# A language-model tower on one core: gate rows multiplied ahead of the up projection, products kept in PSUM, 24 of 33 expert pairs in three-pass form

## The chip, the core and the metric

The kernel runs on one core of one Trainium2 chip. Its engines work side by side, each through its own queue in order: TensorE (PE) multiplies matrices into PSUM, VectorE (DVE) and ScalarE (ACT) work on SBUF and PSUM, GpSimd (POOL) works on SBUF alone, and SyncE (SP) issues DMAs. PSUM has eight banks of 128 rows x 512 floats, and this kernel uses all eight. The metric is the device time of one execution in microseconds (us).

## What is computed

Eight batches of 512 tokens pass through an embedding, one attention-like block and a mixture-of-experts layer. Cut to what matters here:

```python
h = concat([fine_w[ids], softmax(cluster_logits[ids]) @ coarse_w])      # 128 wide
h = h + attn(layernorm(h))     # rms norms, decayed scores, gelu
def ffn(x):                    # x = layernorm(h)
    p = softmax(x @ router_w.T + bias)
    topk_p, topk_i = top_k(p, 6)                  # of 64 experts, capacity-limited
    out = sum over chosen experts e: gate[e] * ((silu(x @ w_gate[e].T) * (x @ w_up[e].T)) @ w_down[e].T)
    return out + shared experts' mean             # 2 shared experts, each 64 wide
h = h + ffn(layernorm(h))
```

The kernel computes all 64 routed experts for every token and multiplies by a gate that is zero where an expert was not chosen.

## The kernel before, in words

Experts are taken in pairs, two times 64 hidden rows on the 128 partitions: pair 0 holds the two shared experts, pairs 1 to 32 the routed ones. One batch is a sequence of 33 iterations, one per pair p, written out on every engine by the functions `pe_sequence`, `act_sequence`, `dve_sequence` and `pool_sequence`. There is no scheduler: the order on each engine is the order of the Python code.

For pair p, PE makes the gate projection (three matmuls into `bank_g`, L481 to L483: high x high, low x high, high x low halves, fp32r) and the up projection (three into `bank_u`). ACT takes silu of the gate bank into `hid` (`act_silu`, L623). DVE multiplies by the up bank (`dve_up`, L881), POOL multiplies by the gate rows, one gate per token, that a DMA has spread over the partitions (L1040). Four iterations later (`LAG`) PE multiplies with the down weights into `bank_y` (`down`). There are two forms of this. In the plain form (even pairs) it is one fp32 matmul from `hid` (L467), which the hardware runs as two records. In the split form (odd pairs) ACT first copies `hid` rounded to fp32r into `hid_hi` (`act_hi`, L629), DVE subtracts to get the rest, `hid_lo` (`dve_lo`, L887), and PE makes three fp32r matmuls (L461, L462, L464).

While the pairs of batch b pass, the steps of the next batches stand between them, at iterations fixed by the tables `DVE_AT`, `PE_AT`, `ACT_AT` and `POOL_AT`: the attention and router of batch b+1 (the "late" steps) and the embedding of batch b+2 (the "early" ones). Those of which the text speaks:

- iteration 6: DVE `scores` (L725), which PE's `state` matmuls (L378) wait for;
- iterations 9 and 10: ACT `squares` (L593); iteration 10: ACT's exp of the cluster logits (early), which puts an activation table load before and after it;
- iteration 11: DVE `xn2` (L746), which PE's transposes `xn2_t` (L396) of iteration 12 wait for;
- iteration 17: DVE `h2` and the statistics after it; iteration 18: POOL `inv3` (L1016); iteration 19: DVE `x3` (L769); iteration 20: PE's transposes of it (L414);
- iterations 23 to 30: the router. PE's matmul is at 23, the logits on DVE (L779 to L785) and ACT's exp with its two table loads at 24, probabilities, top 6 and gates on DVE at 26 to 29, PE's transposes at 30.

Batches 0 to 6 have late steps within their sequence, batches 0 to 5 also early ones, the last has neither. In batches 1 to 5 POOL also issues four gathers, at iterations 1 to 4.

A bank is used again when its reader is done: the gate bank of pair p waits for the silu of p-2, and the up bank for `up_used` of p-2.

## Time and profile before

| what | value |
|---|---|
| median of 3 runs | 717.83 us (716.76 to 718.17) |
| span of the profiled execution | 716.0 us |
| PE busy | 692.8 us, 97% of the span |
| DVE busy | 523.4 us, 73% |
| POOL busy | 466.5 us, 65% |
| ACT busy | 350.6 us, 49% |
| granted TensorE clock, mean | 0.995 |

The only time known of the profiled execution is its span, 716.0 us from its first to its last instruction; the median of the runs is 1.8 us above that. Busy time of PE overlaps from one matmul to the next, so distances between starts tell more than durations do.

### The profile page before, as it was taken

How to read it: one execution, taken by the hardware profiler on the slowest of the kernel's cores; microseconds unless marked ns; L12 is line 12 of the kernel's file. 1: busy time of each engine (PE TensorE's matmuls, PEld its weight loads, DVE VectorE, ACT ScalarE, POOL GpSimd, SP SyncE). 2: the span in 40 equal slices, each digit the busy share in tenths (PEclk: the TensorE clock that was granted, in tenths of full speed). 3: DMA queues.
4: the chain of work that ended last, by engine and by line, in shares of the span. 5: the costliest groups of instructions: out<-in, count | busy, mean ns of one | idle time of the engine just before them, and what ended most of it. 6: DMA issues, size and time to landing. Idle time of an engine off the chain costs nothing.

```text
span 716.0 us, 9975 instructions
## 1 busy us (share of the span) xinstructions
PE 692.8 (97%) x3133; PEld 524.7 (73%) x3133; DVE 523.4 (73%) x1074; ACT 350.6 (49%) x609; POOL 466.5 (65%) x345
## 2 busy tenths in 40 slices
PE   7788899999999999999999999999999999999998
PEld 7666677777777777777777777777777777777775
DVE  5677686987768867887769877788678766674444
ACT  3543455446454374445553474544745435534432
POOL 5035477776677767685676776676775656676664
PEclk9999999999999999999999999999999999999999
DMA  5504232243323333333333433333333433334431
GB/s 204 226 1 128 71 118 104 85 133 105 111 106 114 114 108 99 120 113 102 118 103 101 128 103 103 118 110 109 114 105 102 125 103 105 115 112 124 138 123 60
DMA packets 48869, 80.17 MB, mean 112 GB/s; under 512 B 9520, under 2 KB 13744, under 8 KB 48816
## 3 DMA queue, kind: packets, MB, share of 16 engines
q1 hardware_dynamic: 47792, 77.44, 33.4%
q0 software_dynamic: 1024, 2.10, 1.2%
q8 instruction: 25, 0.41, 0.2%
q14 instruction: 28, 0.23, 0.1%
HBM read 76.35 MB, written 3.15 MB: 111 GB/s over the span
## 4 chain that ended last, share of the span: by engine, by line
PE 88%; DVE 4%; issue 3%; POOL 2%; ACT 1%; DVEq 0%; POOLq 0%
PE bank_y L467 16%; PE bank_g L481 8%; PE bank_g L482 8%; PE bank_g L483 8%; PE bank_u L483 8%; PE bank_u L481 8%; PE bank_u L482 8%; PE bank_y L464 4%; PE bank_y L462 4%; PE bank_y L461 4%; POOL hid L1040 1%; PE bank_f L408 1%; PE bank_f L386 1%; PE bank_f L402 1%; PE bank_f L445 1%
## 5 line engine op out<-in xcount | busy, mean ns | idle before, releaser
L1040 POOL TENSOR_TENSOR hid<-hid,gate_rows 128x512 f32<-128x512 f32 x256 | 374.2, 1470 | 195.4 <-DVE hid L881 193.0
L623 ACT ACTIVATE hid<-bank_g 128x512 f32<-128x512 f32 x264 | 156.6, 599 | 264.4 <-PE bank_g L483 261.8
L881 DVE TENSOR_TENSOR hid<-hid,bank_u 128x512 f32<-128x512 f32 x264 | 178.7, 681 | 128.3 <-PE bank_u L483 78.2
L481 PE MATMUL bank_g<-x_hi,gate_hi 128*128 128x512 f32 x264 | 142.9, 541 | 0.0
L467 PE MATMUL bank_y<-hid,w_down 128*128 128x512 f32 x272 | 138.7, 591 | 0.0
L887 DVE TENSOR_TENSOR hid_lo<-hid,hid_hi 128x512 fp32r<-128x512 f32 x128 | 110.2, 861 | 2.4 <-ACT hid_hi L629 2.4
L482 PE MATMUL bank_g<-x_hi,gate_lo 128*128 128x512 f32 x264 | 104.5, 396 | 0.0
L483 PE MATMUL bank_g<-x_lo,gate_hi 128*128 128x512 f32 x264 | 104.5, 396 | 0.0
L481 PE MATMUL bank_u<-x_hi,up_hi 128*128 128x512 f32 x264 | 103.9, 393 | 0.1
L483 PE MATMUL bank_u<-x_lo,up_hi 128*128 128x512 f32 x264 | 103.8, 393 | 0.0
L482 PE MATMUL bank_u<-x_hi,up_lo 128*128 128x512 f32 x264 | 103.8, 393 | 0.0
L629 ACT ACTIVATE hid_hi<-hid 128x512 fp32r<-128x512 f32 x128 | 80.3, 628 | 5.5 <-POOL hid L1040 4.8
L481 PEld LDWEIGHTS bank_g<-x_hi,gate_hi 128*128 128x128 f32 x264 | 50.1, 190 | 24.1 <-issue 19.2
L482 PEld LDWEIGHTS bank_g<-x_hi,gate_lo 128*128 128x128 f32 x264 | 50.2, 190 | 23.9 <-issue 19.2
L467 PEld LDWEIGHTS bank_y<-hid,w_down 128*128 128x128 f32 x272 | 51.1, 188 | 11.3
L481 PEld LDWEIGHTS bank_u<-x_hi,up_hi 128*128 128x128 f32 x264 | 49.8, 189 | 12.4 <-DVE hid L881 0.6
L482 PEld LDWEIGHTS bank_u<-x_hi,up_lo 128*128 128x128 f32 x264 | 49.8, 189 | 11.8
L483 PEld LDWEIGHTS bank_g<-x_lo,gate_hi 128*128 128x128 f32 x264 | 49.7, 188 | 11.6
L483 PEld LDWEIGHTS bank_u<-x_lo,up_hi 128*128 128x128 f32 x264 | 49.8, 189 | 11.1
L461 PE MATMUL bank_y<-hid_hi,down_hi 128*128 128x512 f32 x128 | 51.3, 401 | 0.0
L464 PE MATMUL bank_y<-hid_lo,down_hi 128*128 128x512 f32 x128 | 50.8, 397 | 0.0
L462 PE MATMUL bank_y<-hid_hi,down_lo 128*128 128x512 f32 x128 | 50.6, 395 | 0.0
(209 smaller groups left out, 857.1 us busy)
## 6 DMA issues: line engine op xcount, KB each, us to landing
gate_rows<-gates_dram SPq DMA_DIRECT2D x512, 128.0 KB, 2.9
w_down<-down_t_dram SPq DMA_DIRECT2D x3, 704.0 KB, 14.5
out_dram<-later SPq DMA_DIRECT2D x7, 256.0 KB, 3.1
hid<-gate_t_dram SPq DMA_DIRECT2D x2, 704.0 KB, 5.8
gates_dram<-gates_t SPq DMA_DIRECT2D x8, 128.0 KB, 2.2
gate_rows<-up_t_dram SPq DMA_DIRECT2D x1, 704.0 KB, 5.7
later<-up_t_dram SPq DMA_DIRECT2D x1, 704.0 KB, 9.9
raw<-gate_t_dram SPq DMA_DIRECT2D x1, 704.0 KB, 11.0
```

The source lines that it names most:

```text
L461: pe.matmul(y, down_hi[:, j, :], hid_hi[:, k, :], start=False, stop=False)
L462: pe.matmul(y, down_lo[:, j, :], hid_hi[:, k, :], start=False, stop=False)
L464: pe.matmul(y, down_hi[:, j, :], hid_lo[:, k, :], start=False, stop=False).then_inc(sem("down_done"), 1)
L467: pe.matmul(y, w_down[:, p, :], hid[:, slot(par, p), :], start=(p == 0), stop=(p == PAIRS - 1)).then_inc(sem("down_done"), 1)
L481: pe.matmul(o, w_hi[name][:, p, :], x3_hi[par][:, :], start=True, stop=False)
L482: pe.matmul(o, w_lo[name][:, p, :], x3_hi[par][:, :], start=False, stop=False)
L483: pe.matmul(o, w_hi[name][:, p, :], x3_lo[par][:, :], start=False, stop=True).then_inc(sem("pe_" + name), 1)
L623: act.activation(hid[:, slot(par, p), :], bank_g[(p + par) % 2][:, :], ACT.Silu).then_inc(sem("silu"), 1)
L629: act.activation(hid_hi[:, (p // 2) % SPLIT_RING, :], hid[:, slot(par, p), :], ACT.Copy)\
L881: dve.tensor_tensor(hid[:, s, :], hid[:, s, :], bank_u[(p + par) % 2][:, :], ALU.mult)\
L887: dve.tensor_tensor(hid_lo[:, k, :], hid[:, slot(par, p), :], hid_hi[:, k, :].bitcast(F32), ALU.subtract)\
L1040: pool.tensor_tensor(hid[:, s, :], hid[:, s, :], gate_rows[:, row, :], ALU.mult)\
```

## The change

Twenty-four pairs instead of sixteen take the split form: all but 0 to 4, 17, 25, 27 and 29. For these pairs the order of the two products is turned round: POOL multiplies the silu by the gate rows as soon as the silu is there, without the up bank, and DVE then multiplies that by the up bank and writes the product back into the same bank (`dve_product`). ACT rounds it from there to `hid_hi`, DVE subtracts from there to `hid_lo`. The up bank of a split pair is therefore held until `hid_lo` is made; there are three up banks instead of two, and one accumulator `bank_y` instead of two. The first down matmul of a batch waits for the copy of the last batch's result, moved from ACT's iteration 5 to 4. `hid_hi` and `hid_lo` have three slots instead of two. The step `x1` goes from DVE to ACT, with a bias column that POOL makes in two small operations. Some SBUF tensors are merged to make room.

```diff
-SPLIT_LAG, SPLIT_RING = 2, 2
-SPLITS = PAIRS // 2
+SPLIT_RING = 3
+PLAIN_PAIRS = (0, 1, 2, 3, 4, 17, 25, 27, 29)
+SPLIT_PAIRS = tuple(p for p in range(PAIRS) if p not in PLAIN_PAIRS)
...
-        bank_u = [bank(f"bank_u{i}") for i in range(2)]
-        bank_y = [bank(f"bank_y{i}") for i in range(2)]
+        bank_u = [bank(f"bank_u{i}") for i in range(3)]
+        bank_y = bank("bank_y")
...
+        def split_slot_freed(b, p):
+            n = SPLITS * b + split_index(p) - SPLIT_RING
+            return PAIRS * (n // SPLITS) + SPLIT_PAIRS[n % SPLITS] + 1 if n >= 0 else 0
...
+            if p == 0:
+                wait(pe, "ffn_t", b)
...
+            for name, o in (("gate", bank_g[q % 2][:, :]), ("up", bank_u[q % 3][:, :])):
+                if name == "gate":
+                    wait(pe, "silu", q - 1)
+                else:
+                    b3, p3 = pairs_back(b, p, 3)
+                    if b3 is not None and is_split(p3):
+                        pe.wait_ge(sem("hid_lo"), split_count(b3, p3))
+                    elif b3 is not None:
+                        pe.wait_ge(sem("up_used"), plain_count(b3, p3))
...
+            if p == ACT_AT["x1"]:
+                act.wait_ge(sem("shift1"), b + 1)
+                wait(act, "x2", b)
+                for t in range(TILES):
+                    last = act.activation(x1[:, t, :], emb[par][:, t, :], ACT.Identity,
+                                          bias=shift1[:, t:t + 1], scale=inv1[:, 0, t:t + 1])
...
+        def act_hi(act, b, p):
+            act.wait_ge(sem("product"), split_count(b, p))
+            wait(act, "down_done", split_slot_freed(b, p))
+            act.activation(hid_hi[:, split_slot(b, p), :], bank_u[(PAIRS * b + p) % 3][:, :], ACT.Copy)\
...
-                if p >= SPLIT_LAG and is_split(p - SPLIT_LAG):
-                    act_hi(act, b, par, p - SPLIT_LAG)
+                b1, p1 = pairs_back(b, p, 1)
+                if b1 is not None and is_split(p1):
+                    act_hi(act, b1, p1)
...
+        def dve_product(dve, b, p):
+            q = PAIRS * b + p
+            dve.wait_ge(sem("gated"), q + 1)
+            dve.wait_ge(sem("pe_up"), q + 1)
+            u = bank_u[q % 3][:, :]
+            dve.tensor_tensor(u, hid[:, slot(b % 2, p), :], u, ALU.mult).then_inc(sem("product"), 1)
...
+        def dve_split(dve, b, p):
+            b2, p2 = pairs_back(b, p, 2)
+            if b2 is not None and is_split(p2):
+                dve_lo(dve, b2, p2)
+            b1, p1 = pairs_back(b, p, 1)
+            if b1 is not None and is_split(p1):
+                dve_product(dve, b1, p1)
...
             for p in range(PAIRS):
+                dve_split(dve, b, p)
...
-                if p >= AHEAD - 1 or not first:
+                if (p >= AHEAD - 1 or not first) and not is_split(p):
                     dve_up(dve, b, par, p)
-                if p >= SPLIT_LAG and is_split(p - SPLIT_LAG):
-                    dve_lo(dve, b, par, p - SPLIT_LAG)
...
-                pool.wait_ge(sem("up_used"), q + 1)
+                if is_split(p):
+                    pool.wait_ge(sem("silu"), q + 1)
+                else:
+                    pool.wait_ge(sem("up_used"), plain_count(b, p))
```

How this stands on the engines is shown at three places. The first is DVE at iterations 10 and 11 of batch 3. Before, with L893 the output of batch 2, L881 the products of pairs 10 and 11 with the up bank, L746 the step `xn2`, L887 the rest of pair 9:

```order
L881 TENSOR_TENSOR hid<-hid,bank_u1 128x512 [waits pe_up,silu]
L887 TENSOR_TENSOR hid_lo<-hid,hid_hi 128x512 [waits hid_hi]
L893 TENSOR_TENSOR later<-bank_f0,later 128x512 [waits stored,pe_out]
L881 TENSOR_TENSOR hid<-hid,bank_u0 128x512 [waits pe_up,silu]
L746 TENSOR_SCALAR xn<-shared,inv2 128x128 [waits inv2]
L746 TENSOR_SCALAR xn<-shared,inv2 128x128 x3
```

and in the changed kernel, where L941 makes `hid_lo` of pairs 8 and 9, L936 the products of pairs 9 and 10, and L792 is `xn2`:

```order
L941 TENSOR_TENSOR hid_lo<-bank_u2,hid_hi 128x512 [waits hid_hi]
L936 TENSOR_TENSOR bank_u0<-hid,bank_u0 128x512 [waits pe_up,gated]
L956 TENSOR_TENSOR later<-bank_f0,later 128x512 [waits stored,pe_out]
L941 TENSOR_TENSOR hid_lo<-bank_u0,hid_hi 128x512 [waits hid_hi]
L936 TENSOR_TENSOR bank_u1<-hid,bank_u1 128x512 [waits pe_up,gated]
L792 TENSOR_SCALAR xn<-shared,inv2 128x128 [waits inv2]
L792 TENSOR_SCALAR xn<-shared,inv2 128x128 x3
```

`xn2` stood behind a product that waits for the silu of pair 10 and the up bank; it now stands behind the `hid_lo` of pair 9 and a product that waits for `gated`, POOL's multiplication of pair 10.

The second place is ACT at iterations 9 and 10 of a batch with early steps. Before, L623 is the silu (of pairs 9, then 10 and 11), L629 `hid_hi` of pair 7, L593 the squares, L612 the exp:

```order
L623 ACTIVATE hid<-bank_g0 128x512 [waits down_done,pe_gate]
L629 ACTIVATE hid_hi<-hid 128x512 [waits down_done,gated]
L593 ACTIVATE shared,ss2<-shared 128x128 [waits x2]
L593 ACTIVATE shared,ss2<-shared 128x128
L612 ACT_TABLE_LOAD
L612 ACTIVATE lg<-lg 128x256 [waits cluster_logits]
L623 ACT_TABLE_LOAD [waits down_done]
L623 ACTIVATE hid<-bank_g1 128x512 [waits pe_gate]
L623 ACTIVATE hid<-bank_g0 128x512 [waits down_done,pe_gate]
```

In the changed kernel L675 is the silu, L681 `hid_hi` (of pairs 8 and 9), L645 the squares, L664 the exp:

```order
L675 ACTIVATE hid<-bank_g0 128x512 [waits down_done,pe_gate]
L681 ACTIVATE hid_hi<-bank_u2 128x512 [waits down_done,product]
L645 ACTIVATE shared,ss2<-shared 128x128 [waits x2]
L645 ACTIVATE shared,ss2<-shared 128x128
L664 ACT_TABLE_LOAD
L664 ACTIVATE lg<-lg 128x256 [waits cluster_logits]
L675 ACT_TABLE_LOAD [waits down_done]
L675 ACTIVATE hid<-bank_g1 128x512 [waits pe_gate]
L681 ACTIVATE hid_hi<-bank_u0 128x512 [waits down_done,product]
L675 ACTIVATE hid<-bank_g0 128x512 [waits down_done,pe_gate]
```

The `hid_hi` before the squares is that of pair 8 instead of pair 7, and one of pair 9 stands between the silus of pairs 10 and 11.

The third place is DVE at iterations 17 to 19. Before, L764 ends the statistics of `h2`, L881 is the product of pairs 17, 18 and L769 is `x3`:

```order
L764 TENSOR_SCALAR var3<-mv3 128x4 [waits mv3]
L881 TENSOR_TENSOR hid<-hid,bank_u1 128x512 [waits pe_up,silu]
L887 TENSOR_TENSOR hid_lo<-hid,hid_hi 128x512 [waits hid_hi]
L868 BN_AGGR mv1<-bn1 128x2 [waits bn1]
L868 BN_AGGR mv1<-bn1 128x2 x3
L872 TENSOR_SCALAR var1<-mv1 128x4 [waits mv1]
L873 TENSOR_SCALAR var1<-mv1 128x4
L881 TENSOR_TENSOR hid<-hid,bank_u0 128x512 [waits pe_up,silu]
L769 TENSOR_SCALAR xn<-later,mv3,inv3 128x128 [waits inv3]
```

In the changed kernel L927 is the plain product of pair 17, L936 that of pair 18, L815 `x3`:

```order
L810 TENSOR_SCALAR var3<-mv3 128x4 [waits mv3]
L927 TENSOR_TENSOR hid<-hid,bank_u2 128x512 [waits pe_up,silu]
L941 TENSOR_TENSOR hid_lo<-bank_u1,hid_hi 128x512 [waits hid_hi]
L914 BN_AGGR mv1<-bn1 128x2 [waits bn1]
L914 BN_AGGR mv1<-bn1 128x2 x3
L918 TENSOR_SCALAR var1<-mv1 128x4 [waits mv1]
L919 TENSOR_SCALAR var1<-mv1 128x4
L936 TENSOR_TENSOR bank_u0<-hid,bank_u0 128x512 [waits pe_up,gated]
L815 TENSOR_SCALAR xn<-later,mv3,inv3 128x128 [waits inv3]
```

The instruction ahead of `x3` waits for POOL's multiplication of pair 18, which stands behind `inv3` in POOL's queue.

## Rows read from the trace of the kernel before

**Rows 1.** The page, part 4: shares of the chain that ended last.
```profile
PE 88%; DVE 4%; issue 3%; POOL 2%; ACT 1%; DVEq 0%; POOLq 0%
```

**Rows 2.** Windows: one batch (busy us by engine, clock, DMA share, GB/s).
```profile
389.94:472.98 83.04, 82.55 (x367) 62.07 (x366) 65.02 (x131) 43.01 (x75) 57.74 (x43) 1.00 0.36 110
```

**Rows 3.** Timeline of PE, pairs 9 to 11: start, us, engine, line, operation.
```profile
333.53 0.40 PE L461 MATMUL bank_y<-hid_hi,down_hi 128*128 128x512 f32 x1
...
334.23 0.39 PE L481 MATMUL bank_g<-x_hi,gate_hi 128*128 128x512 f32 x1
...
335.60 1.02 PE L467 MATMUL bank_y<-hid,w_down 128*128 128x512 f32 x2
...
336.69 0.40 PE L482 MATMUL bank_g<-x_hi,gate_lo 128*128 128x512 f32 x1
```

**Rows 4.** Groups of instructions: busy us, mean ns | idle before.
```profile
L881 DVE TENSOR_TENSOR hid<-hid,bank_u 128x512 f32<-128x512 f32 x264 | 178.7, 681 | 128.3 <-PE bank_u L483 78.2 <-ACT hid L623 48.7
...
L887 DVE TENSOR_TENSOR hid_lo<-hid,hid_hi 128x512 fp32r<-128x512 f32 x128 | 110.2, 861 | 2.4 <-ACT hid_hi L629 2.4
...
L774 DVE TENSOR_TENSOR x_lo<-bank_f,x_hi 128x512 fp32r<-128x512 f32 x8 | 5.5, 692 | 6.1 <-ACT x_hi L604 6.1
...
L604 ACT ACTIVATE x_hi<-bank_f 128x512 fp32r<-128x512 f32 x8 | 4.7, 593 | 0.0
```

**Rows 5.** Timeline of ACT, iteration 10: squares, table load, silus of pairs 10, 11.
```profile
334.06 0.30 ACT L593 ACTIVATE shared<-shared 128x128 f32<-128x128 f32 x1
...
334.76 1.28 ACT L612 ACT_TABLE_LOAD   x1
336.05 0.42 ACT L612 ACTIVATE lg<-lg 128x256 f32<-128x256 f32 x1
...
337.78 1.09 ACT L623 ACTIVATE hid<-bank_g 128x512 f32<-128x512 f32 x2
```

**Rows 6.** Timelines of DVE and PE, iterations 11 and 12: xn2 and its transposes.
```profile
339.02 1.93 DVE L746 TENSOR_SCALAR xn<-shared,inv 128x128 f32<-128x128 f32 x4
...
341.23 0.60 PE L396 MATMUL bank_f<-ident,xn 128*128 128x128 f32 x4
```

**Rows 7.** Timelines of four engines, iterations 16 to 20: silu, h2, gate multiplication, inv3, x3, transposes.
```profile
351.07 0.60 ACT L623 ACTIVATE hid<-bank_g 128x512 f32<-128x512 f32 x1 [0.97 <-PE bank_g L483]
...
353.50 0.75 DVE L752 SCALAR_TENSOR_TENSOR h<-bank_f,op_mul,shared 128x512 f32<-128x512 f32 x1 [0.99 <-PE bank_f L408]
...
356.57 1.66 POOL L1040 TENSOR_TENSOR hid<-hid,gate_rows 128x512 f32<-128x512 f32 x1 [2.70 <-DVE hid L881]
358.18 1.01 POOL L1016 TENSOR_TENSOR inv<-var,neg_half 128x4 f32<-128x4 f32 x1
...
359.23 2.09 DVE L769 TENSOR_SCALAR xn<-h,mv,inv 128x128 f32<-128x128 f32 x4 [0.33 <-POOL inv L1016]
...
361.96 0.60 PE L414 MATMUL bank_f<-ident,xn 128*128 128x128 f32 x4
```

**Rows 8.** Timelines of PE, DVE and ACT, iterations 23 to 26: router, silu 24, gate 26.
```profile
368.83 1.00 PE L419 MATMUL bank_f<-cols,xn_t 128*128 128x64 f32 x8
...
369.86 0.42 DVE L779 TENSOR_TENSOR turns<-bank_f,rows 128x256 f32<-128x256 f32 x1
...
370.78 0.44 DVE L785 TENSOR_TENSOR turns<-turns,rstat 128x256 f32<-128x256 f32 x1
...
372.98 1.09 ACT L623 ACTIVATE hid<-bank_g 128x512 f32<-128x512 f32 x2
...
374.04 0.39 PE L481 MATMUL bank_g<-x_hi,gate_hi 128*128 128x512 f32 x1
```

**Rows 9.** Timelines of POOL, DVE and PE, iterations 4 to 6: gate multiplication, scores, state.
```profile
321.38 1.29 POOL L1040 TENSOR_TENSOR hid<-hid,gate_rows 128x512 f32<-128x512 f32 x1
...
324.22 0.74 DVE L725 TENSOR_TENSOR shared<-bank_f,decay_mask 128x256 f32<-128x256 f32 x2
...
325.06 0.91 PE L378 MATMUL bank_f<-z,shared 128*128 128x128 f32 x6 [0.49 <-issue]
```

More of the change, by code:

```diff
@@ L18 @@
+import itertools
 from contextlib import ExitStack
@@ L463, in down @@
                 pe.wait_ge(sem("hid_lo"), split_count(b, p))
-                pe.matmul(y, down_hi[:, j, :], hid_lo[:, k, :], start=False, stop=False).then_inc(sem("down_done"), 1)
+                pe.matmul(y, down_hi[:, j, :], hid_lo[:, k, :], start=False, stop=(p == PAIRS - 1)).then_inc(sem("down_done"), 1)
             else:
@@ L675, in _ @@
                     act.wait_ge(sem("w_down"), 16 * (PAIRS // CHUNK))
-                    act.activation(down_hi[:, :, :], odd_pairs(w_down), ACT.Copy).then_inc(sem("down_hi"), 1)
+                    for j, pairs in split_runs():
+                        last = act.activation(down_hi[:, j, :], w_down[:, pairs, :], ACT.Copy)
+                    last.then_inc(sem("down_hi"), 1)
                     act.wait_ge(sem("sigmoid"), 1)
@@ L681, in _ @@
             last = BATCHES - 1
-            for p in range(PAIRS - SPLIT_LAG, PAIRS):
-                if is_split(p):
-                    act_hi(act, last, 1, p)
+            if is_split(PAIRS - 1):
+                act_hi(act, last, PAIRS - 1)
             act.wait_ge(sem("down_done"), PAIRS * BATCHES)
@@ L982, in _ @@
             last = BATCHES - 1
-            for p in range(PAIRS - SPLIT_LAG, PAIRS):
-                if is_split(p):
-                    dve_lo(dve, last, 1, p)
+            dve_split(dve, last, PAIRS)
+            if is_split(PAIRS - 1):
+                dve_lo(dve, last, PAIRS - 1)
             dve.wait_ge(sem("stored"), 16 * BATCHES)
```

108 lines of the change are left out of this document (58 added, 50 removed).

## The prediction

> **What bounds the kernel now.** I read three views in this order: the chain of waits, to see which engine it stays on; the busy times of one batch, to see what that engine loses; then the timelines around every place where PE takes something from another engine, to see how late that could come. The chain is on PE for 88% of the span, with no second engine over 4% [rows 1]. A middle batch takes 83.04 us and PE works in 82.55 of them, at the full granted clock, the 2.4 GHz level; DVE works 65 and POOL 58 [rows 2]. So a microsecond of PE work is worth a microsecond, and so is a microsecond of PE waiting, which nothing gives back. The change pays in the first and has to be charged for the second.
>
> **What it saves.** A split down product is three matmuls 0.23 us apart (333.53 to 334.23), 0.70 in all. A plain one and the first gate matmul behind it take 335.60 to 336.69, that is 1.09, less 0.23 is 0.86 [rows 3]. Twenty-four pairs are split instead of sixteen, and each of the eight saves 0.16: 8 x 8 batches x 0.16 = 10.2 us.
>
> **What the engines get.** Eight `hid_lo` more per batch go to DVE, and four `x1` leave it. A `hid_lo` took 0.86 on average with both inputs in SBUF; with one input in PSUM the nearest row is `x3_lo`, 0.69 [rows 4]. I use 0.69 for the product and for `hid_lo`. [...] The product writes PSUM, which no row of DVE shows; the nearest is the same operation into SBUF, 0.68, and I let it lie between 0.55 and 0.86. In a run of split pairs DVE cannot take the next product before the last `hid_lo`, and that waits for ACT: product 0.69, rounding 0.59 [rows 4], 0.60 from one DVE start to the next, hand-overs of 0.04 (inv3 ends at 359.19, `x3` starts at 359.23 [rows 7]): 1.96 us per pair against PE's 2.08 (nine matmuls). It holds, by 0.12; at 0.86 it would lose 0.05 a pair, some 10 us over 192 pairs. The four `x1` lie in ACT's idle time of iteration 5 at 0.30 each (nearest row, the squares [rows 5]); POOL's two small operations are well under its 25 idle us of a batch [rows 2]. The copy of `bank_y` lies beside the gate and up matmuls of pair 4. I cost these at zero; `x1` uncovered would be 1.2 us in seven batches, 8 us.
>
> **What it charges: order.** DVE takes the product of pair p-1 first thing in iteration p and waits there for POOL. Before, it needed silu and the up bank only. After a silu's end come POOL (1.29 alone [rows 9]), the product (0.60 to the next start) and two hand-overs, so a step of iteration p can start 2.0 us after silu p-1, where it started 0.6 after it. The steps and PE's uses of them keep their iterations, so each use must have that much slack. I take a middle batch, put the changed kernel's PE on the old clock, and look at the four uses.
>
> - *`xn2_t`, iteration 12.* `hid_hi` of pair 8 has the slot of pair 5, whose down product is the last of iteration 9 and ends 0.16 after 334.23 [rows 3]. So it starts at 334.44, the squares at 334.94 instead of 334.06 (ACT starts every 0.5), and the exp and its two table loads push the silu of pair 10 from 337.78 to 338.66 [rows 5]. It ends 339.26, POOL 340.60, product from 340.65, `xn2` from 341.25. It took 1.93 with one of its four pieces stopped by POOL: end 343.2. PE used it at 341.23 [rows 6], now 341.07: 2.1 late. With none stopped I put it at 1.2 (four at the 0.30 of a 128x128 piece on ACT [rows 5]), 1.4 late; each piece behind one more POOL operation gives 3.7. I take 1.9, in the six batches with early steps: 11.4 us.
> - *`x3_t`, iteration 20.* Silu 16 ends at 351.67 [rows 7], POOL 353.01, product, `h2` from 353.66 at the earliest instead of 353.50. To the end of inv3 it was 5.69, now 5.32, as POOL is not stopped (1.66 to 1.29). Then `x3` does not start at 0.04 after it, but behind gate multiplication and product of pair 18, another 1.29 + 0.05 + 0.60: 360.9 instead of 359.23. With 2.09 it ends at 363.0; PE wants it at 361.96 [rows 7] less three shorter down products, 361.48. Late by 1.5; by 0.6 if `x3` runs in 1.2; by 2.9 if gelu's table loads in iteration 14 still hold up `h2`. I take 1.7 in six batches, 1.0 in batch 6: 11.2 us.
> - *Router to gates, iterations 24 to 30.* The down product of pair 19 ends at 368.99 [rows 8] and frees the slot for `hid_hi` 22: 369.04 to 369.63, `hid_lo` 22, product 23 at 370.28, logits from 370.88 instead of 369.86. Silu 24 goes from 372.98 to 374.0, ends 374.6; gate 26 wants it at 374.04 less 0.16: 0.77 late. Behind silu 24 stands `hid_hi` 23, then `hid_lo` 23 (to 375.83), which the up bank of pair 26 waits for: 1.3 late in all. In iterations 26 to 29 DVE has three more such steps between the `hid_lo`, and I add 1.05, between 0 and 2. 2.35 in seven batches: 16.5 us.
> - *`state`, iteration 6.* POOL, full of gathers, ends pair 4 at 322.67, then pair 5 at 324.01; the product puts `scores` from 324.22 to 324.66, and PE already waits for them [rows 9]. 0.45 in batches 1 to 5: 2.2 us; between 0 and 4.
>
> The exp and its load in the first of these chains start 1.29 apart [rows 5]. The Trainium skill (ScalarE: Activation LUTs, "What ACT_TABLE_LOAD costs") has 1.28 for the load and 1.38 more for a drain, which would put silu 10 and 24 later still. The trace has no such drain, so it decides against the rule; the sum above goes by the row.
>
> **Sum.** -10.2 + 11.4 + 11.2 + 16.5 + 2.2 = +31.1. On the profiled span of 716.0 that is 747.1; the median of the runs lies 1.8 above the span, so **749 us**. The lower bounds (1.4 x 6, 0.6 x 7, 0.77 x 7, 0) come to 18.0 - 10.2 = +8, 726 us; the upper (3.7 x 6, 2.9 x 7, 3.3 x 7, 4) to 69.6 - 10.2 = +59, 777.
>
> **Rivals.**
> - *All of it hidden: faster.* If DVE, free of POOL's stops, is early enough at all four uses, only the saving stays: 717.8 - 10.2 = 708. For it: three up banks give PE a lead of three pairs, and the DVE-ACT loop fits. Against it: this needs slack of 1.4 us at each use, and the trace has 0.3 at `xn2` (ends 340.95, used 341.23) and 0.6 at `x3` (361.32, 361.96). It decides where the waits of a batch come to less than 10.2 / 7, about 1.5 us. Chance 0.15, for all of 708 to 716.4.
> - *The waits overlap: a small loss.* If a wait at one use gives the other engines the lead that the next use needs, the lower bounds hold, about 726. For it: after each wait of PE the others catch up. Against it: the uses are 8 and 4 iterations apart, and each chain starts from PE's own work. 0.20 for 716.4 to 733, 0.04 of it within 0.2% of before.
> - *POOL stops every piece: a larger loss.* POOL now starts at the silu, so its operations come back to back where `xn2` and `x3` run, and each of the four pieces waits for one: upper bounds, about 777. For it: one piece of `xn2` was stopped even before, and `x3` took 2.09 [rows 6, 7]. The Trainium skill (SBUF — State Buffer, "SBUF: two separate sides") calls the shared ports an exclusive lock, held for the whole instruction; the rows bear that out. Against it: while PE waits, POOL soon has nothing left to do. 0.13, above 766.
> - The forecast, 733 to 766: 0.52.
>
> **Chances and range.** A measurement of this kernel can tell about 0.2% from no change. Faster 0.15, within 0.2% 0.04, slower 0.81. The range is 717 to 775: it leaves out the first rival and some 0.05 of the third.
>
> **What would show it.** Right: a middle batch of some 87 to 89 us; idle time of PE before `xn2_t`, `x3_t` and `state` and before the gate and up matmuls of pairs 26 and 29, put down to DVE and ACT; `hid_lo` at 0.69 throughout; POOL's multiplication near 1.3. Wrong: PE busy through a batch of 82 us; or waits in the runs of split pairs without steps, which the last batch shows alone: there PE should take 1.3 us less than now, and if it takes more, the product into PSUM is dearer than I think.

## The result, and the profile after

The changed kernel takes **781.9 us** (median of 4 runs, 781.1 to 784.0) against 718.0 beside it: 1.089 times as long, 95% interval 1.087 to 1.092. Forecast were 749, with a range from 717 to 775. The sign and the kind of loss were right, the size was not: 64 us instead of 31.

The profiled execution has a span of 781.8 us, 65.8 more than before. Its chain of waits no longer stays on PE; a quarter of it is POOL, and four fifths of that is one line, the gate multiplication (L1108, 20% of the chain) [rows 1]:

```profile
PE 35%; issue 33%; POOL 25%; DVE 4%; ACT 2%; DMA 1%; POOLq 0%; SPq 0%; DVEq 0%; ACTq 0%
```

One middle batch and the last one, in the columns of [rows 2], and below them the last batch of the kernel before. The middle batch has grown from 83.04 to 92.24; in it PE is at the full clock (1.00), and idle for 8.4 us. The last batch, which has no steps, has grown from 69.67 to 70.10.

```profile
429.11:521.35 92.24, 83.86 (x375) 62.80 (x374) 65.06 (x135) 48.25 (x87) 51.70 (x45) 1.00 0.34 99
702.22:772.32 70.10, 69.17 (x284) 52.87 (x283) 39.07 (x61) 33.59 (x57) 42.17 (x33) 1.00 0.45 126
```

```profile
636.67:706.34 69.67, 69.67 (x277) 51.51 (x276) 32.12 (x50) 27.96 (x49) 48.11 (x33) 1.00 0.40 126
```

The groups that answer to [rows 4], from the page: POOL's multiplication, `hid_hi`, `hid_lo` and the product. All four take what was forecast (1.3, 0.59, 0.69, 0.69), so none of these durations explains the loss. What has changed is the last column, the idle time ahead of them: before, DVE's product never waited for POOL and `hid_lo` waited 2.4 us in all for ACT; now it is 70.9 and 115.1.

```profile
L1108 POOL TENSOR_TENSOR hid<-hid,gate_rows 128x512 f32<-128x512 f32 x256 | 328.3, 1295 | 272.5 <-ACT hid L675 182.3
L681 ACT ACTIVATE hid_hi<-bank_u 128x512 fp32r<-128x512 f32 x192 | 114.8, 598 | 213.5 <-DVE bank_u L936 188.8
L941 DVE TENSOR_TENSOR hid_lo<-bank_u,hid_hi 128x512 fp32r<-128x512 f32 x192 | 132.1, 688 | 117.2 <-ACT hid_hi L681 115.1
L936 DVE TENSOR_TENSOR bank_u<-hid,bank_u 128x512 f32<-128x512 f32 x192 | 132.1, 688 | 71.6 <-POOL hid L1108 70.9
```

What PE waited for (total us, times, longest): `xn2` (L432), the up banks (L525), `x3` (L450), the gate banks, and for `state` (L414). The number of times is telling: 8 is once a batch, at one place.

```profile
PE bank_f L432 <- DVE xn L792: 17.3, 8, 2.5
PE bank_u L525 <- DVE hid_lo L941: 15.9, 34, 1.0
PE bank_f L450 <- DVE xn L815: 10.3, 8, 1.4
PE bank_g L525 <- ACT hid L675: 7.4, 12, 0.8
PE bank_f L414 <- issue: 7.0, 6, 1.2
```

The next table goes by place. PE's second gate matmul starts once in each pair; the table has the distances between these starts in one middle batch, summed over the stretches around each use. "Best" is the run e18 below, in which no stretch of such a batch has a wait of any size.

| us, middle batch | before | after | best |
|---|---|---|---|
| pairs 0 and 1 | 4.77 | 6.00 | 4.78 |
| 4 to 7 (`state`) | 12.99 | 14.01 | 12.63 |
| 11 and 12 (`xn2_t`) | 5.20 | 8.92 | 5.19 |
| 19 and 20 (`x3_t`) | 4.78 | 6.84 | 4.66 |
| 21 to 32 (router, gates) | 27.31 | 29.28 | 26.99 |
| the rest | 27.97 | 27.18 | 27.01 |
| sum | 83.03 | 92.23 | 81.26 |

**The largest loss, at `xn2`.** Timelines of ACT, DVE, POOL and PE in iterations 8 to 12 of one batch; a row with x4 is four instructions together, [ ] the idle time before it.

```profile
458.80 0.60 ACT L681 ACTIVATE hid_hi<-bank_u 128x512 fp32r<-128x512 f32 x1 [0.86 <-PE bank_y L502]
...
459.99 1.28 ACT L664 ACT_TABLE_LOAD   x1
461.29 0.42 ACT L664 ACTIVATE lg<-lg 128x256 f32<-128x256 f32 x1
...
463.02 0.60 ACT L675 ACTIVATE hid<-bank_g 128x512 f32<-128x512 f32 x1
```

```profile
465.02 0.70 DVE L936 TENSOR_TENSOR bank_u<-hid,bank_u 128x512 f32<-128x512 f32 x1 [0.19 <-POOL hid L1108]
465.62 3.34 DVE L792 TENSOR_SCALAR xn<-shared,inv 128x128 f32<-128x128 f32 x4
```

```profile
463.69 2.55 POOL L1108 TENSOR_TENSOR hid<-hid,gate_rows 128x512 f32<-128x512 f32 x2 [2.20 <-ACT hid L675]
466.19 1.27 POOL L1073 TENSOR_TENSOR shared<-emb,shared 128x512 f32<-128x512 f32 x1
467.42 1.27 POOL L1108 TENSOR_TENSOR hid<-hid,gate_rows 128x512 f32<-128x512 f32 x1
```

```profile
469.01 0.66 PE L432 MATMUL bank_f<-ident,xn 128*128 128x128 f32 x4 [2.47 <-DVE xn L792]
```

The chain ahead of `xn2` is the one forecast, link by link: `hid_hi` 8 waits for a slot that PE frees, the exp and its two table loads (1.28 each) follow, the silu, POOL, the product. `xn2` starts 0.60 after the product, as it should. But it takes 3.34 instead of 1.93 [rows 6]. Its four pieces run 465.62 to 466.32, then to 467.54, to 468.76 and to 468.96; each of the first three ends 0.08 after an operation of POOL does (466.24, 467.46, 468.68), and only the last takes its own 0.27. POOL, which now starts at the silu, has four operations back to back, `hx` (L1073) among them, and here one piece of DVE gets through per operation.

**The loss that was not foreseen, at pair 0.** DVE, POOL and PE at the end of one batch:

```profile
427.14 0.70 DVE L936 TENSOR_TENSOR bank_u<-hid,bank_u 128x512 f32<-128x512 f32 x1 [2.04 <-POOL hid L1108]
...
427.92 1.27 DVE L874 TENSOR_TENSOR_SCAN taken<-one_col,taken_end,bank_f 64x512 f32<-64x512 f32 x1
429.23 0.69 DVE L879 SCALAR_TENSOR_TENSOR gates_t<-taken,bank_f 64x512 f32<-64x512 f32 x1
429.95 0.69 DVE L941 TENSOR_TENSOR hid_lo<-bank_u,hid_hi 128x512 fp32r<-128x512 f32 x1
```

```profile
424.58 3.79 POOL L1108 TENSOR_TENSOR hid<-hid,gate_rows 128x512 f32<-128x512 f32 x3 [2.28 <-DVE hid L927]
```

```profile
430.69 0.50 PE L525 MATMUL bank_u<-x_hi,up_hi 128*128 128x512 f32 x1 [0.96 <-DVE hid_lo L941]
```

POOL takes its pairs in order, and the plain pair 29 still has to wait for DVE (2.28), so 30 and 31 are late; the product of 30 waits 2.04 for POOL, the scan `taken` and `gates_t` of iteration 31 stand behind it, and `hid_lo` 30, which frees the up bank of pair 0, behind those. The last batch waits there too, though it has no late steps, since the scan is the end of the batch before it.

At `x3` and `state` the shorter form of the same is seen [rows 7, 9]: `x3` starts behind a product (489.22) and takes 1.46; `scores` start at 448.38, behind a product that waited 3.51 for POOL, full of gathers, and PE's `state` waits 1.16.

```profile
489.22 0.70 DVE L936 TENSOR_TENSOR bank_u<-hid,bank_u 128x512 f32<-128x512 f32 x1 [2.18 <-POOL hid L1108]
489.82 1.46 DVE L815 TENSOR_SCALAR xn<-later,mv,inv 128x128 f32<-128x128 f32 x4
```

```profile
447.77 0.70 DVE L936 TENSOR_TENSOR bank_u<-hid,bank_u 128x512 f32<-128x512 f32 x1 [3.51 <-POOL hid L1108]
448.38 0.75 DVE L771 TENSOR_TENSOR shared<-bank_f,decay_mask 128x256 f32<-128x256 f32 x2
```

```profile
449.22 0.91 PE L414 MATMUL bank_f<-z,shared 128*128 128x128 f32 x6 [1.16 <-issue]
```

### The profile page after: what moved, and what is told of

Read it like the earlier page. It is cut to its first block, busy times and chain, and to the rows that moved or that the text cites. A ratio compares the mean times of both kernels' runs of the same rounds, so it can differ in the third digit from the quotient of the medians.

```text
span 781.8 us, 10340 instructions
## 1 busy us (share of the span) xinstructions
PE 705.5 (90%) x3197; PEld 535.8 (69%) x3197; DVE 530.0 (68%) x1110; ACT 395.5 (51%) x709; POOL 417.7 (53%) x361
## 4 chain that ended last, share of the span: by engine, by line
PE 35%; issue 33%; POOL 25%; DVE 4%; ACT 2%; DMA 1%; POOLq 0%; SPq 0%; DVEq 0%; ACTq 0%
POOL hid L1108 20%; PE bank_y L505 6%; PE bank_u L525 3%; PE bank_u L527 3%; PE bank_u L526 3%; PE bank_g L525 3%; PE bank_g L527 3%; PE bank_g L526 3%; PE bank_y L502 2%; PE bank_y L500 2%; PE bank_y L499 2%; DVE taken L874 1%; POOL inv L1082 1%; POOL shared L1073 1%; POOL inv L1076 1%
## 5 line engine op out<-in xcount | busy, mean ns | idle before, releaser
L1108 POOL TENSOR_TENSOR hid<-hid,gate_rows 128x512 f32<-128x512 f32 x256 | 328.3, 1295 | 272.5 <-ACT hid L675 182.3
L681 ACT ACTIVATE hid_hi<-bank_u 128x512 fp32r<-128x512 f32 x192 | 114.8, 598 | 213.5 <-DVE bank_u L936 188.8
L941 DVE TENSOR_TENSOR hid_lo<-bank_u,hid_hi 128x512 fp32r<-128x512 f32 x192 | 132.1, 688 | 117.2 <-ACT hid_hi L681 115.1
L675 ACT ACTIVATE hid<-bank_g 128x512 f32<-128x512 f32 x264 | 157.7, 598 | 92.2 <-PE bank_g L527 89.1
L936 DVE TENSOR_TENSOR bank_u<-hid,bank_u 128x512 f32<-128x512 f32 x192 | 132.1, 688 | 71.6 <-POOL hid L1108 70.9
L525 PE MATMUL bank_g<-x_hi,gate_hi 128*128 128x512 f32 x264 | 132.3, 501 | 7.4 <-ACT hid L675 7.4
L525 PE MATMUL bank_u<-x_hi,up_hi 128*128 128x512 f32 x264 | 109.2, 414 | 16.1 <-DVE hid_lo L941 15.9
L525 PEld LDWEIGHTS bank_u<-x_hi,up_hi 128*128 128x128 f32 x264 | 49.8, 189 | 45.0 <-DVE hid_lo L941 35.9
L499 PE MATMUL bank_y<-hid_hi,down_hi 128*128 128x512 f32 x192 | 76.7, 399 | 0.0
L500 PE MATMUL bank_y<-hid_hi,down_lo 128*128 128x512 f32 x192 | 76.5, 398 | 0.0
L502 PE MATMUL bank_y<-hid_lo,down_hi 128*128 128x512 f32 x192 | 76.1, 396 | 0.0
L505 PE MATMUL bank_y<-hid,w_down 128*128 128x512 f32 x144 | 73.4, 591 | 0.0
L525 PEld LDWEIGHTS bank_g<-x_hi,gate_hi 128*128 128x128 f32 x264 | 50.2, 190 | 30.6 <-ACT hid L675 13.3
L526 PEld LDWEIGHTS bank_g<-x_hi,gate_lo 128*128 128x128 f32 x264 | 50.3, 190 | 17.5 <-issue 12.0
L927 DVE TENSOR_TENSOR hid<-hid,bank_u 128x512 f32<-128x512 f32 x72 | 49.1, 682 | 12.9 <-PE bank_u L527 12.8
## 6 DMA issues: line engine op xcount, KB each, us to landing
w_down<-down_t_dram SPq DMA_DIRECT2D x3, 704.0 KB, 14.5
```

The lines of the kernel that those rows point to most:

```text
L499: pe.matmul(y, down_hi[:, j, :], hid_hi[:, k, :], start=False, stop=False)
L500: pe.matmul(y, down_lo[:, j, :], hid_hi[:, k, :], start=False, stop=False)
L502: pe.matmul(y, down_hi[:, j, :], hid_lo[:, k, :], start=False, stop=(p == PAIRS - 1)).then_inc(sem("down_done"), 1)
L505: pe.matmul(y, w_down[:, p, :], hid[:, slot(par, p), :], start=(p == 0), stop=(p == PAIRS - 1)).then_inc(sem("down_done"), 1)
L525: pe.matmul(o, w_hi[name][:, p, :], x3_hi[par][:, :], start=True, stop=False)
L526: pe.matmul(o, w_lo[name][:, p, :], x3_hi[par][:, :], start=False, stop=False)
```

## Experiments

Three theories: **order** (steps, and roundings that free a bank, stand on DVE behind a product that waits for POOL), **port** (pieces on DVE are stopped by POOL's operations, which now come back to back), **number** (24 split pairs are more than DVE and ACT carry). Times are medians, each against the kernel before on the same chip, which took 716.8 to 717.9 in all of them. A difference to the changed kernel (781.9) is one between chips, so some 1 us of it means nothing.

**e1, the step ahead of the split work.**
```diff
-                dve_split(dve, b, p)
                 if p == DVE_AT["result"] and not first:
                     dve_out(dve, b - 1, 1 - par)
...
                     dve_early(dve, b + 2, par, p, b // 2 + 2)
+                dve_split(dve, b, p)
```


> In each iteration DVE does its step first, and hid_lo of pair p-2 and the product of pair p-1 behind it; nothing else differs from the changed kernel (782). Theory A, order: the steps start late because they stand behind a product that waits for POOL. Then the waits at xn2_t, x3_t and state go for the most part and the time falls by 30 to 45, to 737 to 752; a part may come back as waits of the up banks for hid_lo, since the product now stands behind the step. Theory B, port: what makes xn2 and x3 late is that each of their pieces waits for one of POOL's back-to-back multiplications. Then an earlier start by some 0.7 us gives back only that, about 1 to 1.5 us a batch: 770 to 775. Theory C, number: 24 split pairs are more than DVE and ACT carry. Then the waits only move to the up banks and the time stays at 778 to 786.

762.2 us, 19.7 less, in none of the three ranges: the waits at pair 0 (4.75 in the table's first row) and `state` (12.63) are gone and those at `xn2` (6.46) and `x3` (5.78) about halved or better, but the router's stretch has grown to 31.42, and PE waits for up banks:

```profile
PE bank_u L525 <- DVE hid_lo L941: 34.2, 52, 2.6
```

Order is a cause, but it cannot be cured by turning it round: what frees a bank now stands behind the step.

**e2, POOL's `hx` away from `xn2`.**
```diff
-POOL_AT = dict(inv2=10, hx=12, inv3=18, inv1=20)
+POOL_AT = dict(inv2=10, hx=14, inv3=18, inv1=20)
```


> One number: POOL's operation hx moves from iteration 12 to 14, so that it no longer stands between the gate multiplications of pairs 11 and 12 while DVE has xn2. Theory B, port: one of the three pieces of xn2 that POOL stops is then not stopped, or the gate multiplication of pair 12 comes in its place 1.3 earlier; if not stopped, xn2 ends 1.3 to 1.9 earlier in six batches, 770 to 775. Theory A, order: the start of xn2 is what counts and it doesn't move; 779 to 783. If the next multiplication steps in hx's place, B gives 779 to 783 too, and the trace tells: xn2 then still has three pieces that end with a POOL operation.

767.3 us, 14.5 less for one number of a table, and less than the 770 to 775 that the port theory had allowed. `xn2` starts as late as it did (0.60 after the product) and takes 1.29: DVE, then POOL, whose next multiplication comes at 455.74, when `xn2` has ended.

```profile
453.98 1.29 DVE L792 TENSOR_SCALAR xn<-shared,inv 128x128 f32<-128x128 f32 x4
```

```profile
452.06 2.54 POOL L1108 TENSOR_TENSOR hid<-hid,gate_rows 128x512 f32<-128x512 f32 x2 [2.20 <-ACT hid L675]
455.74 1.29 POOL L1108 TENSOR_TENSOR hid<-hid,gate_rows 128x512 f32<-128x512 f32 x1 [1.14 <-ACT hid L675]
```

Port, at this use: one piece is still stopped, and two come free, not one, since the multiplication behind `hx` no longer meets them. PE's wait for `xn2` falls from 17.3 to 3.1 us in all.

**e3, the old order of the product, all else as changed.**
```diff
-            act.wait_ge(sem("product"), split_count(b, p))
+            act.wait_ge(sem("gated"), PAIRS * b + p + 1)
...
-                if is_split(p):
-                    pool.wait_ge(sem("silu"), q + 1)
+                pool.wait_ge(sem("up_used"), q + 1)
```


> All as in the changed kernel (24 split pairs, three up banks, one accumulator, x1 on ScalarE), but the product in the order of before: DVE multiplies with the up rows first, in place in SBUF, POOL multiplies the gate rows behind it, and hid_hi and hid_lo are made from hid in SBUF two iterations later. Theory A, order: the waits at pair 0, xn2, x3 and router vanish, and only the saving of eight split pairs a batch and a prelude 3 to 4 longer are left: 708 to 716. Theory C, number: 24 hid_lo at 0.86 and their ports stop POOL and make the gate multiplications late for the down products: 720 to 745. If the waits stay though the product does not wait for POOL, one accumulator or x1 is their cause: above 760.

729.8 us, 1.017 of before (1.015 to 1.019). The edit turns back several things together: the order of the two products, the rounding from PSUM instead of SBUF, the long hold of the up bank, `hid_hi` one iteration behind instead of two, and the split work at the head of DVE's iterations. The new order makes 52 of the 64 us with all that it brings along; this run does not price the parts. The 24 split pairs still do not pay, and the time lies in the range of the number theory (720 to 745). What is left is a wait at the router (stretch 29.65) and one at `xn2` (5.78). The chain, in three timelines: POOL's `inv1` holds up the gate multiplications of pairs 20 and 21, ACT's `hid_hi` 20 waits 1.68 for POOL, DVE's `hid_lo` 20 waits 1.50 for that, and behind it stand the logits (L822).

```profile
455.27 2.09 POOL L1076 TENSOR_TENSOR inv<-var,neg_half 128x8 f32<-128x8 f32 x1
...
458.03 5.95 POOL L1099 TENSOR_TENSOR hid<-hid,gate_rows 128x512 f32<-128x512 f32 x4
```

```profile
459.35 0.63 ACT L677 ACTIVATE hid_hi<-hid 128x512 fp32r<-128x512 f32 x1 [1.68 <-POOL hid L1099]
```

```profile
460.01 1.10 DVE L938 TENSOR_TENSOR hid_lo<-hid,hid_hi 128x512 fp32r<-128x512 f32 x1 [1.50 <-ACT hid_hi L677]
...
462.74 0.41 DVE L822 TENSOR_TENSOR turns<-bank_f,rows 128x256 f32<-128x256 f32 x1
```

**e4, the new order with 16 split pairs** (`PLAIN_PAIRS`: 0, 1, 2 and the even pairs 4 to 30).

> The changed kernel with 16 to 17 split pairs rather than 24: plain are 0, 1, 2 and then the even pairs 4 to 30, so 17 of 33 are plain and every second pair is split. Theory A, order: every second step still stands behind a product that waits for POOL, and the saving of 10 is lost; steps in an iteration behind a split pair wait as now. If the steps at 11 and 19 (behind pairs 10 and 18, both plain now) have their products out of the way, xn2 and x3 gain, and router (24, behind the split pair 23) does not: 750 to 775. Theory C, number: it is the density of the DVE and ACT work; all waits shrink, 725 to 735. Theory B, port: POOL still works back to back beside xn2: 780 to 790.

755.8 us, where the number theory had 725 to 735. The loss falls place by place: with pair 30 plain none at pair 0 (4.75), with 18 plain none at `x3` (4.76), but behind the split pairs 5 and 23 `state` (14.12) and the router (30.11) are as late as ever, and at `xn2` (6.78) POOL still meets the pieces. Order and port, not number.

**e5 and e6, rounding first, then the step, then the product; e6 with `hx` at 14 as well.**
```diff
-                dve_split(dve, b, p)
+                b2, p2 = pairs_back(b, p, 2)
+                if b2 is not None and is_split(p2):
+                    dve_lo(dve, b2, p2)
...
                     dve_early(dve, b + 2, par, p, b // 2 + 2)
+                b1, p1 = pairs_back(b, p, 1)
+                if b1 is not None and is_split(p1):
+                    dve_product(dve, b1, p1)
```


> Changed kernel, with DVE's order in an iteration: hid_lo of pair p-2, then the step, then the product of pair p-1. With the step ahead of both, PE waited 34 us in 52 places for up banks that hid_lo had not released; a bank is released here before the step. Theory A, order (nothing that waits for POOL may stand ahead of a step, nothing that releases a bank behind one): most of these 34 us go and the steps still start early, 730 to 745. Rival, number: the three up banks are short whatever the order, since product and hid_lo of a pair lie two iterations apart; then the waits stay near 30 us and the time at 755 to 762.

> The order hid_lo, step, product, and POOL's hx in iteration 14 rather than 12. Theory A and B together: hx beside xn2 cost 14 us in the changed kernel; here xn2 starts earlier, when POOL may have the multiplication of pair 10 or 11 in hand, so I expect half of it, 5 to 9 us under the same order with hx at 12. If the order alone brings xn2 clear of its use, hx is worth nothing: within 2.

795.7 and 789.0 us: worse than the changed kernel. My improvement of e1 was wrong. The product is now the last thing in an iteration and the rounding of the same pair the first of the next, so DVE stands idle for ACT's `hid_hi` between them and the step is late by that. In e1 and in the changed kernel the step, where there is one, lies between the two. In all DVE idles 145.5 us for `hid_hi` here, 115.1 in the changed kernel and 90.2 in e1. Without a step a pair takes the 1.96 us that the prediction had worked out, 0.66 of it idle (DVE's timeline of e5), and here a step comes on top:

```profile
476.72 0.69 DVE L941 TENSOR_TENSOR hid_lo<-bank_u,hid_hi 128x512 fp32r<-128x512 f32 x1 [0.66 <-ACT hid_hi L681]
477.33 0.69 DVE L936 TENSOR_TENSOR bank_u<-hid,bank_u 128x512 f32<-128x512 f32 x1
478.68 0.69 DVE L941 TENSOR_TENSOR hid_lo<-bank_u,hid_hi 128x512 fp32r<-128x512 f32 x1 [0.66 <-ACT hid_hi L681]
```

`hx` is worth 6.6 here, as expected.

**e7, e3 with `hid_lo` three iterations behind instead of two** (`pairs_back(b, p, 3)`).

> The order of before with 24 split pairs (729.8), but hid_lo made three iterations behind its pair rather than two; hid_hi stays at two. There PE lost about 1.4 us before the gate matmul of pair 25 and 1.3 before gates_t in seven batches, since hid_lo 20 and 21 stood ahead of the logits on DVE and waited for hid_hi, which waited for POOL. Theory A, order: a hid_lo that waits for nothing holds up no step; these 19 us go for the most part, 711 to 720. Rival, ports: POOL and DVE shut each other out (hid_lo with both inputs in SBUF took up to 1.4 us), whatever the order: 725 to 732.

752.5 us, a miss too: the down product is only four iterations behind, and PE now waits for the rounding itself.

```profile
PE bank_y L502 <- DVE hid_lo L938: 30.5, 37, 1.7
```

**e8, `x1` back on DVE, all else as changed** (the four `tensor_scalar` ahead of `xn_dec`).

> The changed kernel with x1 back on DVE in iteration 5, ahead of xn_dec; all else as changed. The prediction had x1 at zero on both engines. If that holds, only the prelude changes, where four x1 of 0.49 stand ahead of z on ScalarE: 779 to 783. If x1 on ScalarE holds up z and by it state (PE waits 0.7 there in five batches) it gains up to 4: 776 to 779. If the four x1 on DVE hold up scores, by 0.3 to 1.3 each where POOL shuts DVE out, PE waits longer for state: 785 to 795.

798.0 us, 16 more, above all that was expected. DVE's four pieces take 6.84 us there, beside two gathers and four multiplications of POOL; before, one took 728 ns on average, now 1371. The fourth alone takes 4.53: it begins at 451.29, within the second gather, and ends 0.09 after the last of the three multiplications behind that:

```profile
448.98 6.84 DVE L746 TENSOR_SCALAR x<-emb,mv,inv 128x128 f32<-128x128 f32 x4
```

```profile
450.92 1.05 POOL L1056 DMA_INDIRECT emb<-table_dram,idx  x1 [0.16 <-issue]
451.98 3.75 POOL L1104 TENSOR_TENSOR hid<-hid,gate_rows 128x512 f32<-128x512 f32 x3
```

So moving `x1` is a part of the change that pays, in the new order.

**e11, steps first in twelve iterations only** (0, 2, 4, 5, 6, 8 to 11, 19, 24, 31), `hx` at 14.

> The changed kernel with DVE's step ahead of hid_lo and product only in the iterations whose step PE soon needs (0, 2, 4, 5, 6, 8 to 11, 19, 24, 31), as in the changed kernel elsewhere, and hx in iteration 14. Theories A and B together: the waits at pair 0, state, xn2_t and x3_t go (1.2 + 0.7 + 2.7 + 1.6 a batch) without the up-bank waits of iterations 18 to 27 that the order with all steps first brought (some 4 a batch): 732 to 745. If the up-bank waits follow wherever a step goes first: 750 to 760.

752.4 us, the rival's range, though its mechanism is only half there. The waits at pair 0 (4.94) and `state` (12.65) are gone, and a new up-bank wait stands at pair 21 (0.60); but in all PE waits 17.5 us for up banks, against 17.2 in e2 with the same `hx`. The stretches at `x3` (6.73) and the router (29.37) are as long as in the changed kernel.

**e12, e3 with the 16 split pairs of e4.**

> Old order of the product and 16 split pairs, so that what is left of the change is the third up bank, the one accumulator, x1 on ScalarE, vals in the space of xn2_t, the split of w_down in pieces. The prediction had all of these at zero. If so, only a prelude 3 to 4 longer shows: 719 to 723. If one of them costs in every batch: 725 to 740, and the trace tells at which use.

718.3 us, 1.002 of before (1.0005 to 1.003). In the old order the third up bank, the single accumulator, `x1` on ScalarE and the merged tensors together cost next to nothing: in a middle batch 83.35 us against 83.03.

**e13, plain pairs 5, 10, 18, 23, 27, 30 ahead of the steps, in the new order, `hx` at 14.**

> The changed kernel's order, still 24 split pairs, but the plain ones are 5, 10, 18, 23, 27 and 30 in place of 3, 4, 17, 25 and 29 (so that no product that waits for POOL stands ahead of state, xn2, x3, logits, gates and taken), and hx in iteration 14. Theory A, order, place by place: a step waits only where the pair ahead of it is split, so pair 0, state, x3_t and the router's waits go (1.2 + 0.7 + 1.6 + 2.3 a batch) and with hx the most of xn2_t (2.5): 718 to 735. Rival, number: with 24 split pairs DVE and ACT are late anywhere in iterations 5 to 30 and the waits only change place: 755 to 768.

754.7 us, just under the range of the number theory (755 to 768). Pair 0 is cured (4.76), `x3` in part (5.82), `xn2` (7.26) and the router (29.27) are not, and at `state` (13.66) the wait has moved one iteration forward: PE waits 0.97 there for DVE's `turns` (L764). With pair 10 plain no product that waits for POOL stands ahead of `xn2`, and still its four pieces take 3.60, through three multiplications of POOL in a row that began at 446.39:

```profile
446.83 3.60 DVE L792 TENSOR_SCALAR xn<-shared,inv 128x128 f32<-128x128 f32 x4
```

```profile
446.39 3.76 POOL L1108 TENSOR_TENSOR hid<-hid,gate_rows 128x512 f32<-128x512 f32 x3 [2.68 <-DVE hid L927]
```

That is port without order at this use. I had expected the plain pairs and the later `hx` to cure it.

**e15, `xn2` on ScalarE ahead of the silu of pair 11, all else as changed, `hx` at 12.**
```diff
+            if p == XN2_AT:
                act.wait_ge(sem("inv2"), b + 1)
+                for t in range(TILES):
+                    last = act.activation(xn2[:, t, :], x2[:, t, :], ACT.Copy, scale=inv2[:, t:t + 1])
```


> The changed kernel (782) with xn2 made on ScalarE, ahead of the silu of pair 11, rather than on DVE behind the product of pair 10; all else as changed, hx in iteration 12 too. Theory B, port: of the 3.9 us a batch at xn2_t the pieces that POOL stops make 2.0; on ScalarE four pieces of 0.5 end about 3.5 earlier, and the silu of pair 11 comes 1.8 later: PE gets back 2 to 3.9 a batch in six batches, 758 to 770. Theory A alone: xn2 no longer stands behind a product either, so the whole 3.9 go, but nothing is left for the pieces: the same range; the trace tells A from B by the pieces (0.5 each or 1.3). Rival: ScalarE, late at the table loads of iteration 10, is the bound at xn2 on any engine: 776 to 783.

772.0 us, between the two ranges expected. The pieces take 0.40 each, the first three beside a multiplication of POOL (459.77 to 461.06), and the stretch at `xn2` falls from 8.92 to 6.22:

```profile
460.07 1.27 ACT L644 ACTIVATE xn<-shared,inv 128x128 f32<-128x128 f32 x4
```

The stretch alone is worth 2.7 x 6 = 16 us, and ten came out: `x3` takes 0.5 a batch of it, and pair 0 of the first batch started at 55.8 instead of 52.4.

**e9, e10, e14, e16, e17, e18: does the old order pay with 24?** From e3, the plain pairs and POOL's and DVE's tables were moved by what each trace showed to be late: e9 pairs 8, 20, 21, e10 `inv1` at 25, e14 pair 30 and the gates' steps an iteration earlier, e16 pair 28 and `inv1` at 24, where POOL stood idle, e17 pairs 25 and 26, e18 `top` at 27. The lines of e18 that differ from the changed kernel beyond e3's:
```diff
-PLAIN_PAIRS = (0, 1, 2, 3, 4, 17, 25, 27, 29)
+PLAIN_PAIRS = (0, 1, 2, 3, 8, 25, 26, 28, 30)
...
-              h=15, bn1=16, h2=17, bn3=17, mv1=18, x3=19, x3_lo=21, router=24, prob=26, top=27, chosen=28, gates=29,
+              h=15, bn1=16, h2=17, bn3=17, mv1=18, x3=19, x3_lo=21, router=24, prob=26, top=27, chosen=27, gates=28,
...
-POOL_AT = dict(inv2=10, hx=12, inv3=18, inv1=20)
+POOL_AT = dict(inv2=10, hx=12, inv3=18, inv1=24)
```


> The order of before with 24 split pairs (729.8), but other plain pairs: 8, 20 and 21 in place of 4, 17 and 29. The hid_lo of 8, 20 and 21 stood ahead of xn2 and the logits on DVE and waited for POOL. Theory A, order, carried to the old order: what stood ahead of the logits is gone, PE no longer waits at pair 25 and gates_t (2.7 a batch) and less at xn2_t (0.6): 708 to 718. Rival, ports: POOL and DVE shutting each other out delays the same steps whichever pairs are split: 724 to 732.

> As the run with plain pairs 8, 20 and 21, and POOL's inv1 (2.09 us and two small operations) in iteration 25 rather than 20. If POOL's late gate multiplications of pairs 20 to 23 are what still holds up the logits, 3 to 8 us less; if the plain pairs have cured it, no change within 2; a new wait at gates_t (pairs 26 to 28 late in their turn) would make it 3 to 8 more.

> The old order with 24 split pairs, inv1 in iteration 25 (721.4), and two more changes: pair 30 plain in place of 27, so that no late hid_lo stands ahead of xn, and the steps top, chosen and gates an iteration earlier (26, 27, 28). In the run of before these PE waited 1.3 a batch for the gates before gates_t and 0.55 for xn. Theory A: both go, 8 x 1.3 + 7 x 0.5 = 14 us less: 706 to 711, under the kernel before. If the steps only push the gate multiplications of pairs 26 to 28 behind their down products: 716 to 724.

> The old order with 24 split pairs and the gates' steps an iteration earlier (718.1), with POOL's inv1 in iteration 24, where POOL stood idle for 3.9 us behind silu 24 waiting for the router, and pair 28 plain in place of 25, so that its late hid_lo does not stand ahead of taken and xn. PE waited there 0.5 before xn_t, 0.3 and 0.3 for hid_lo of pairs 24 and 26 in every batch: 7 us less, 709 to 713, under the kernel before. If the roundings of pair 25 hold up the gates in their turn: 714 to 719.

> As the run with inv1 in iteration 24 (718.1), with pairs 25 and 26 plain in place of 20 and 21, whose roundings inv1 no longer holds up. PE's waits for hid_lo of pairs 24 to 26 (0.3 + 0.3 + 0.85 a batch) go but for that of 24: 1.2 x 7 = 8 us less, 708 to 713. If the number is what costs, hid_lo 20 and 21 hold up the logits again as with inv1 in iteration 20 (2.7 a batch): 720 to 730.

> The same with the step top in iteration 27 rather than 26, ahead of chosen: the rounding of pair 24 comes 0.9 earlier, and the rest of the wait for it (0.3 a batch) goes if the gates are still in time: 706 to 711. If the gates come late for gates_t, 711 to 716.

722.6, 721.4, 718.1, 718.1, 712.0 and **707.7 us**. e9, e10, e14 and e16 fell short, each time because another rounding or step was late in its turn (the gates ahead of `gates_t` in e9, 1.17, and e10; roundings of pairs 24 to 26, up to 0.71, in e14 and e16); e17 is 0.993 of before (0.991 to 0.994), e18 **0.986 (0.984 to 0.988)**, faster than both kernels. Its middle batch, in which PE never rests, and the longest total of its waits, two of them, at 20 and 63 us, while the program gets under way:

```profile
384.46:465.72 81.26, 81.26 (x374) 63.56 (x373) 66.61 (x135) 48.79 (x87) 61.29 (x44) 1.00 0.37 112
```

```profile
PE bank_f L387 <- DVE xn L746: 4.2, 2, 2.4
```

DVE and POOL shut each other out more than in the changed kernel (`hid_lo` 840 ns, gate multiplication 1560), and it costs nothing. That closes the theory of number for the old order: 24 split pairs fit, and against e12, the same order with 16, they and the moved steps save 10.6 us. No run shows whether 24 can be made to fit in the new order.

## Why the prediction was wrong

- *What bounds the kernel, and that a wait of PE is not given back:* right. PE's bound held in every run; e18 is a kernel with the waits gone.
- *The saving, 10.2:* nearly. In the last batch, which shows it alone where pair 0 doesn't wait (e1, e3), it is 69.67 - 68.85 = 0.82, not 1.28: in a run of split pairs the gate matmuls of neighbours stand 2.11 apart, not 2.08. That is 6.6 in eight batches from this row; e18 against e12 gained 10.6, with the steps in it.
- *Durations and the DVE-ACT loop:* right, 0.69, 0.60 and 1.30. The new order has the same 2.11 a pair as the old in the last batch, so the loop did not bind there; that the product's target in PSUM costs as much as SBUF (688 against 681) was within the bounds.
- *`xn2_t`, 1.9 a batch:* **the step that failed.** The start was right (2.60 after the start of silu 10, forecast 2.59), the length was not: "1.93 with one of its four pieces stopped" was carried over from a kernel in which POOL's operations came one at a time. After, three were stopped, `xn2` took 3.34, and the stretch lost 8.92 - 5.20 = 3.7. That is the upper bound (3.7) that I had given to the third rival with a chance of 0.13; the bound stands there without its working, so that it is met to a tenth is in part luck. Six batches make 22 us instead of 11.4, and batch 6, which I had left out, 1.9 more. e2, e13 and e15 show the cause. The rival's reason against itself, that POOL soon has nothing left while PE waits, was wrong because of `hx`: the silus of pairs 10 and 11 came in a burst behind the table loads, and `hx` filled POOL's time until silu 12 was there (467.30). In e2, without `hx` at that place, POOL does run out (idle for 1.14), and one piece is stopped instead of three.
- *Pair 0:* the other failure, a term at nothing. I looked for steps that PE uses; `taken` is a step that no matmul of its iteration wants, but it stands ahead of the `hid_lo` that frees a bank. 1.2 in seven batches, 8.5 us. e1, e4 and e13 cure it, each in its way.
- *The prelude,* costed at zero, is 4.1 longer (pair 0 starts at 52.36, before at 48.29). About 1.2 of it on ACT and 1.9 on DVE is the split of `w_down`, for 24 pairs in five pieces instead of for 16 in one (1.90 to 3.12 and 2.29 to 4.20), as far as they lie on the path; the rest is not settled, and in other runs pair 0 started between 50.4 and 55.8.
- *`x3_t`, 1.7:* 2.1, within its bounds. *`state`, 0.45:* 1.16 - 0.49 [rows 9] = 0.67, within. *Router, 2.35:* 2.0 against before, 2.3 against e18: the size was right, and so were the places. PE waits for silu 24 before the gate matmul of pair 26 (0.78, forecast 0.77), then before its up matmul and that of pair 29 (0.43):

```profile
504.25 0.51 PE L525 MATMUL bank_g<-x_hi,gate_hi 128*128 128x512 f32 x1 [0.78 <-ACT hid L675]
505.47 0.50 PE L525 MATMUL bank_u<-x_hi,up_hi 128*128 128x512 f32 x1 [0.24 <-DVE hid_lo L941]
```

  That turning the order back would cure it is not shown: e3 loses as much in this stretch, by other waits (1.09 before the gate of 26, 1.22 at `gates_t`).
- *`x1` and the rest at zero:* right in the steady batches for the old order (e12); in the new one `x1` on ACT is worth 16 us, which I hadn't seen.

The excess adds up to within 2 us: `xn2` 12.8, pair 0 8.5, prelude 4.1, saving 3.6, `x3` about 3 and `state` 1.1 are 33, against 65.8 - 31.1 = 34.7. That takes all batches alike, which holds for batches 2 to 5 (9.2 us lost in each); batch 0 lost 6.2, batch 1 10.5, batch 6 7.9 and the end, from the last batch on, 0.3. Of the signs that I had named, the middle batch (92 instead of 87 to 89) spoke against me. "PE in the last batch takes more, so the product is dearer" would have misled: the last batch was longer for pair 0 alone.

The Trainium skill (SBUF — State Buffer, "SBUF: two separate sides") names as holders of the shared lock a DVE operation in a two-port mode, and one with two SBUF inputs against a GpSimd operation that reads SBUF. So the number of SBUF inputs does not decide alone: `xn2` and `x1` read one tensor from SBUF and write SBUF, and the trace has them stopped (0.28 to 1.30; 1371 ns), while the product and `hid_lo`, with PSUM in them, were not (688). That `xn2` and `x1` run in a two-port mode no run here shows. The same section says that ACT's ports never wait, and e15's 0.40 agrees.
